# One transformer layer on one core: batch 2's projections reordered in the first pass, work moved between the first two batches, a projection's first matmul ahead of the shift

## What is computed

```python
qkv = layernorm(x) @ qkv_w.T                    # 16 heads of 8 channels
qb, kb = q, k averaged over blocks of 64 rows   # 8 blocks
c = einsum(qb, kb) * scale                      # block against block, per head
mask = (c >= the largest of each row) | own block
probs = softmax(where(mask, q @ k.T * scale, -inf))
x = x + (probs @ v) @ proj_w.T + proj_b
xf = layernorm(x); logits = xf @ wr + br        # 4 experts, the best 2 count
h = gelu(xf @ w1 + b1); y = h @ w2 + b2         # each expert 128 -> 512 -> 128
x = x + sum over the best two of gate * (y - c_sel + c_sum)
```

## Time and profile before

| | us |
|---|---|
| median of 3 runs | 876.28 |
| lowest, highest | 875.84, 877.91 |
| the profiled execution's own time | 867.59 |
| its span (first to last instruction) | 865.6 |

### The profile page before, as it was taken

How to read it: one execution, slowest core, us unless ns; L and a number is a source line. 1 busy time by engine, 2 the same in 40 slices (tenths; PEclk the granted TensorE clock), 3 DMA queues, 4 the chain that set the end, 5 groups by cost and what they waited for, 6 DMA issues and landing times.

```text
span 865.6 us, 23561 instructions
## 1 busy us (share of the span) xinstructions
PE 811.2 (94%) x9326; PEld 546.7 (63%) x9326; DVE 519.5 (60%) x1526; ACT 469.3 (54%) x772; POOL 174.8 (20%) x176
## 2 busy tenths in 40 slices
PE   2668899999999999999999999999999999999995
PEld 2546666666667666666767676666766666665662
DVE  7655647575665756666675757666575666655321
ACT  1334464755557474655637465554747465563740
POOL 6100411213022121303122031212212130201111
PEclk8776999999999999999999999999999999999998
DMA  5989613737566473736557284646647374650210
GB/s 157 226 229 219 151 62 107 164 129 171 136 162 164 128 180 120 179 116 166 141 165 174 97 177 129 165 125 175 167 121 168 122 174 128 166 129 2 62 62 14
DMA packets 187185, 121.90 MB, mean 141 GB/s; under 512 B 123688, under 2 KB 169648, under 8 KB 187072
## 3 DMA queue, kind: packets, MB, share of 16 engines
q1 hardware_dynamic: 184768, 107.77, 48.2%
q0 software_dynamic: 2304, 12.58, 4.8%
HBM read 78.24 MB, written 42.08 MB: 139 GB/s over the span
## 4 chain that ended last, share of the span: by engine, by line
PE 76%; ACT 10%; issue 4%; DVE 4%; DMA 2%; SPq 2%; POOL 0%; POOLq 0%; ACTq 0%; DVEq 0%
PE y_ps L446 20%; PE o_ps L376 8%; PE s_ps L282 6%; PE s_ps L328 6%; PE s_ps L284 5%; PE s_ps L283 5%; PE s_ps L361 5%; ACT hid L1128 5%; PE o_ps L388 4%; PE v_ps L352 3%; PE a_ps L419 2%; ACT L1085 2%; PE v_ps L408 2%; PE v_ps L446 2%; PE v_ps L400 1%
## 5 line engine op out<-in xcount | busy, mean ns | idle before, releaser
L446 PE MATMUL y_ps<-hid,w2s 128*128 128x512 f32 x480 | 235.1, 600 | 0.0
L1085 ACT ACTIVATE prob<-s_ps 128x1024 f32<-128x1024 f32 x128 | 131.1, 1024 | 131.8 <-PE s_ps L361 131.1
L1128 ACT ACTIVATE hid<-s_ps,b1s 128x512 f32<-128x512 f32 x256 | 171.3, 688 | 41.3 <-PE s_ps L284 38.2
L761 DVE TRANSPOSE_TENSOR_REDUCE rmax<-s_ps 128x16 bf16<-128x512 f32 x256 | 168.1, 698 | 39.4 <-PE s_ps L328 39.3
L1251 POOL TENSOR_TENSOR yT<-yT,gate_cols 128x512 f32<-128x512 f32 x48 | 61.4, 1279 | 293.8 <-DVE gate_cols L865 293.4
L282 PE MATMUL s_ps<-xnhi,w1hi 128*128 128x512 f32 x256 | 113.1, 442 | 1.3
L446 PEld LDWEIGHTS y_ps<-hid,w2s 128*128 128x128 f32 x480 | 83.0, 192 | 43.9 <-issue 40.0
L770 DVE TENSOR_REDUCE nmax<-v_ps 128x64 bf16<-128x256 bf16 x128 | 54.1, 423 | 90.5 <-PE v_ps L352 90.4
L284 PE MATMUL s_ps<-xnhi,w1lo 128*128 128x512 f32 x256 | 101.0, 395 | 0.0
L283 PE MATMUL s_ps<-xnlo,w1hi 128*128 128x512 f32 x256 | 100.6, 393 | 0.0
L376 PEld LDWEIGHTS o_ps<-prob,vaug 128*32 128x32 f32 x4096 | 64.5, 111 | 55.2 <-issue 42.4
(11 more groups left out here) (163 smaller groups left out, 1042.5 us busy)
## 6 DMA issues: line engine op xcount, KB each, us to landing
gate_cols<-gates SPq DMA_DIRECT2D x64, 256.0 KB, 4.1
kv_table<-stage SPq DMA_DIRECT2D x16, 768.0 KB, 4.1
keys<-kv_table SPq DMA_DIRECT2D x48, 256.0 KB, 6.6
qdiag<-q_table SPq DMA_DIRECT2D x128, 96.0 KB
kv_chosen<-selected SPq DMA_DIRECT2D x32, 384.0 KB, 4.4
keys<-kv_chosen SPq DMA_DIRECT2D x96, 128.0 KB, 3.3
q_table<-qpair SPq DMA_DIRECT2D x16, 512.0 KB, 2.9
xs<-in_x SPq DMA_DIRECT2D x16, 256.0 KB, 5.6
```

What stands on the lines that cost most here:

```text
L446: ins = pe.matmul(dst[:], w2s[:, n, :], hid[:, n, :], start=(c == 0), stop=(c == C - 1))
L761: v.tensor_reduce(rmax[m % 2][:, :, half * P // 2:half * P // 2 + HH].rearrange("p k h -> p h k"), s_ps[m % 2][:, half * N:(half + 1) * N] ...
L1085: act.activation(prob[m % 2][:].rearrange("p h s -> p (h s)"), s_ps[m % 2][:], ACT.Exp, scale=SCALE).then_inc(exped, 1)
L1128: act.activation(hid[:, k, :], up_ps[up_bank(k)], ACT.Gelu, bias=b1s[:, k:k + 1]).then_inc(gelued, 1)
```

## The change

In `early(0)`: batch 2's k is projected ahead of the steps, q in step 3 and v in step 6 (before: q, then k in step 2, then v in step 4). The readers move with them: DVE takes `ksum` in u = 0, the low half of k in u = 2, `qsum` and the block product's input in u = 4, `qlo` in u = 6; ACT copies k's high half behind step 1 (now with a wait for `k_summed`), q's behind step 4, v behind step 6. `values(0, 0)` moves ahead of `shift(0, 0)`. `begin(1)` (batch 1's first scores and values) and `a_products(2)` now come at the end of step 7, ahead of `weighted(0, 7)`; before, both weighted sums 6 and 7 came first. DVE's `a_select(2)` moves from step 6 to step 7, and `block_max(1, 0)` stands behind it.

In `early(1)`: three of the four `bn_stats` of batch 0's second mean move to step 2, batch 0's route sum to step 7. POOL's `split_w1` now waits for `xn2_done`, that is, until DVE has written batch 0's normalised rows.

On SP: batch 1's `place_q`, both halves, is issued ahead of `put_q(2)` and `put_table(2)`. `take_own(b)` for b >= 3 also waits until POOL has added the second of the sums of two batches back (`summed`).

In the 13 passes: the first matmul of each projection is issued ahead of the step's `shift`, the other two stay where all three were.

```diff
@@ project
+            def project_begin(b, part):
+                was, part_of = bank_a.next(part, b), slice("qkv".index(part) * D, ("qkv".index(part) + 1) * D)
+                pe.wait_ge(bank_a.free, was)
+                pe.matmul(a_ps[:], wqkvhi[:, part_of], xnhi[:], start=True, stop=False)
...
@@ early
-                    if m + 1 < M and u >= 1:
+                    if u == 0:
+                        values(b, m)
+                    elif m + 1 < M:
                         values(b, m + 1)
...
-                    if b == 0 and m in (2, 4):
-                        project(2, "k" if m == 2 else "v")
-                    if b == 0 and m == 6:
+                    if b == 0 and m in (3, 6):
+                        project(2, "q" if m == 3 else "v")
+                    if b == 0 and m == 7:
+                        begin(1)
                         a_products(2)
...
-            project(2, "q")
+            project(2, "k")
             early(0)
-            begin(1)
...
@@ the passes
+                    if ahead and m in stages[:3]:
+                        project_begin(b + 1, "qkv"[stages.index(m)])
                     shift(b, m)
...
                     if ahead and m in stages[:3]:
-                        project(b + 1, "qkv"[stages.index(m)])
+                        project_end("qkv"[stages.index(m)])
...
@@ DVE
+                    if u == 10:
+                        c_stats_begin(0)
...
-                    if b == 0 and m == 6:
+                    if b == 0 and m == 7:
                         tied = a_select(2)
+                        block_max(1, 0)
...
@@ POOL
             inverse(0, mv2, veps2, rstd2, mean2_done, rstd2_done)
+            g.wait_ge(xn2_done, 1)
             split_w1(0)
...
@@ SP
+                if b >= 3:
+                    s.wait_ge(summed, (E - 1) * (b - 3) + 2)
...
+            place_q(1, 0)
+            place_q(1, 1)
             put_q(2)
-            place_q(1, 0)
             put_table(2, bank_a)
-            place_q(1, 1)
```

More of the change, by code:

```diff
@@ L193, in layer @@
         table_out, q_out = sem("table_out"), sem("q_out")
-        q_high, q_summed, own_valued = sem("q_high"), sem("q_summed"), sem("own_valued")
+        q_high, q_summed, k_summed, own_valued = sem("q_high"), sem("q_summed"), sem("k_summed"), sem("own_valued")
         own_k_in, sel_v_in = ([sem(f"{n}{i}") for i in range(2)] for n in ("own_k_in", "sel_v_in"))
@@ L305, in project, with project_end @@
                 exact(dst[:], wqkvhi[:, part_of], wqkvlo[:, part_of], xnhi[:], xnlo[:]).then_inc(of.full, 1)
+            def project_begin(b, part):
+                was, part_of = bank_a.next(part, b), slice("qkv".index(part) * D, ("qkv".index(part) + 1) * D)
+                pe.wait_ge(bank_a.free, was)
+                pe.matmul(a_ps[:], wqkvhi[:, part_of], xnhi[:], start=True, stop=False)
+            def project_end(part):
+                part_of = slice("qkv".index(part) * D, ("qkv".index(part) + 1) * D)
+                pe.matmul(a_ps[:], wqkvhi[:, part_of], xnlo[:], start=False, stop=False)
+                pe.matmul(a_ps[:], wqkvlo[:, part_of], xnhi[:], start=False, stop=True).then_inc(bank_a.full, 1)
             def a_products(b):
@@ L506, in early @@
                     if u == 0:
-                        values(b, m)
                         values(b, m + 1)
@@ L704, in a_q_low, with a_k_early @@
                 v.tensor_tensor(qlo, a_ps[:], qhi.bitcast(F32), ALU.subtract).then_inc(bank_a.free, 1)
-            def a_k_sum(b):
-                v.wait_ge(k_high, b + 1)
-                return step(v.tensor_reduce(ksum[:], block_ap(a_ps[:]), AXX, ALU.add))
+            def a_k_early(b):
+                v.wait_ge(bank_a.full, bank_a.at["k", b])
+                v.tensor_reduce(ksum[:], block_ap(a_ps[:]), AXX, ALU.add).then_inc(k_summed, 1)
             def a_k_rest(b):
@@ L732, in a_qk @@
             def a_qk(total):
-                v.wait_ge(dve_step, total)
+                if total:
+                    v.wait_ge(dve_step, total)
                 v.tensor_tensor(qk[:], heads_of(qsum[:]).broadcast_to([P, M, M]),
@@ L802, in c_stats, with c_stats_begin, c_stats_end @@
                 mean(x2[b % N2], stats2, mv2, mean2_done)
+            def c_stats_begin(b):
+                of = bank_of("proj", b, T - 2)
+                v.wait_ge(of.free, of.at["proj", b, T - 2])
+                for k in range(T - 1):
+                    ins = v.bn_stats(stats2[:, k, :], x2[b % N2][:, k, :])
+                step(ins)
+            def c_stats_end(b):
+                of = bank_of("proj", b, T - 1)
+                v.wait_ge(of.free, of.at["proj", b, T - 1])
+                v.wait_ge(dve_step, step(v.bn_stats(stats2[:, T - 1, :], x2[b % N2][:, T - 1, :])))
+                for k in range(T):
+                    ins = v.bn_aggr(mv2[:, k, :], stats2[:, k, :])
+                ins.then_inc(mean2_done, 1)
             def c_rows(b):
@@ L931, in vector @@
                     if u == 0:
+                        a_k_early(2)
+                    if u == 2:
+                        v.wait_ge(k_high, 3)
+                        a_k_rest(2)
+                    if u == 4:
                         a_q_early(2)
-                    if u == 2:
+                        v.wait_ge(q_summed, 1)
+                        v.wait_ge(k_summed, 1)
+                        a_qk(0)
+                    if u == 6:
                         a_q_low(2)
-                    if u == 3:
-                        k_total = a_k_sum(2)
-                    if u == 4:
-                        a_k_rest(2)
-                        v.wait_ge(q_summed, 1)
-                        a_qk(k_total)
+                    if u == 10:
+                        c_stats_begin(0)
                     if m + 1 < M:
@@ L946, in vector @@
                         o_rows(*pair_at(u - 3))
-                    if b == 0 and m == 6:
+                    if b == 0 and m == 7:
                         tied = a_select(2)
+                        block_max(1, 0)
                     if b == 1 and m == 3:
-                        c_stats(0)
+                        c_stats_end(0)
                     if b == 1 and m == 4:
@@ L954, in vector @@
                         c_split(0)
+                    if b == 1 and m == 7:
                         c_route(0)
-                if b == 0:
-                    block_max(1, 0)
             ranked = c_logits(0)
@@ L1065, in a_q_high, with a_k_high @@
                 act.copy(qhi, a_ps[:]).then_inc(q_high, 1)
-            def a_k_high(b):
+            def a_k_high(b, k_total=False):
                 act.wait_ge(bank_a.full, bank_a.at["k", b])
+                if k_total:
+                    act.wait_ge(k_summed, 1)
                 act.wait_ge(table_out, 16 * b)
@@ L1152, in scalar @@
                     if b == 0 and m == 1:
+                        a_k_high(2, k_total=True)
+                    if b == 0 and m == 4:
                         a_q_high(2)
-                    if b == 0 and m == 2:
-                        a_k_high(2)
-                    if b == 0 and m == 4:
+                    if b == 0 and m == 6:
                         a_v(2)
+                    if b == 0 and m == 7:
+                        values(1, 0)
                     if b == 1 and m == 0:
@@ L1162, in scalar @@
                 o_copy(b, T - 1)
-                if b == 0:
-                    values(1, 0)
             o_columns(1, T - 2)
```

## The result

| | before | after |
|---|---|---|
| median, us | 876.06 (873.52 to 877.91, 4 runs) | 865.20 (864.75 to 865.26, 4 runs) |
| ratio, 95% interval | 1 | 0.9869 (0.984 to 0.9897) |
| profiled execution, own time | 867.59 | 865.26 |
| its span | 865.6 | 863.2 |

The change gains 10.9 us, 2.3 more than the 8.7 forecast and inside the range. But the two profiled executions differ by only 2.4 us. Before's profiled execution took 867.59 us, less than any timed run of that kernel here, the fastest of which took 870.51; after's took what its timed runs take. So the first question is which of the two traces tells of the runs that were timed.

A forecast was written before the change was run, and what follows sets the result against it. PE's own list bounds the kernel from the third pass on, waits and low clock the first two batches. First part 3.5 plus split 5.2 = 8.7 us, from 876.28 to 867.6 us; range 861.5 to 873.7.

The forecast's parts named there:

- first part: Start, batches 0 and 1: its edits, net of w2's lateness and the low clock, gain 3.5 us (1 to 6).
- the split: 13 passes: each projection's first matmul ahead of the shift gains 0.40 us a pass, 5.2 us in all.
- k first: Batch 1's start: the 6.7 us `qpair` wait goes, PE waits 3.8 us for queries, scores at 64.5, before 72.28.
- The select behind begin(1): Batch 1's first scores to next row maximum: 4.5 us instead of 2.21, a loss; row maximum at 69.0.
- w1's split later: Batch 1's step 5: DVE's normalisations no longer slowed by POOL; 2.6 us plus 1.1 of clock, 3.7 gained.
- w2 as the limit: At `bias_out`: w2's load lands at 100.8, PE stands 3.6 us, gain there 5.6 us instead of 9.2.
- rival A: At `bias_out`: w2 in time, start keeps 9.2 us, 861.9; middle (w2 at 99, stand 1.5 us) 864.2; chance 0.2.
- The clock: Behind PE's stand for w2: low clock for 4.2 us of PE work costs 2.1 us (1.2 to 2.7).
- SP's wait: Passes: own keys go out 3.9 us later, chosen keys have 3.8 us to spare; effect 0.
- The rival C: Passes: chosen keys come too late after SP's wait, first scores wait; 883.2 at 5 us delay; chance 0.06.
- B: Passes gain nothing, moved matmul's long slot or DVE's chain: 872.8 (chance 0.18); longer slot loses 2.6 us, 875.4 (0.08).
- D: Start gains nothing: batch 1's queries late, clock low, w2 later by 3 us; total 871; chance 0.1.

The follow-up runs named there:

- before's second trace: The unchanged kernel before, profiled once more: own time 875.94 us.
- first part alone: After with projections whole behind the shift and own keys sent for as in before, so neither edit of the passes: 870.09 us, 0.9933 of before.
- short hold: POOL's gather of chosen rows held until DVE has written head group 6's row maxima: before 864.96 us, after 856.18, after with projection whole 858.77.

## Why the prediction was right, and where it was not

The forecast was -8.7 us and the change brought -10.9. It was carried from one trace to the median, and that trace, as found above, was not typical. Most parts went the way that was forecast (w2 did not), but that the sum came out near is in part luck: the first part brought some 2 to 3 us more than its 3.5, the split 1.4 to 2.6 less than its 5.2, and about 2.5 us of shorter stalls stand in no term.

- **k first.** Right. The `qpair` wait went, ACT's copy of k is at 43.85 (forecast 43.5), and what came is the forecast wait for the queries: 4.2 us against 3.8, scores at 65.38 against 64.5. But its value was overstated: 6.7 us was the long case, 3.3 the usual one.
- **The select behind begin(1).** Right: row maximum at 69.69 against 69.0.
- **w1's split later.** Right in mechanism, undersized: 3.7 us forecast, of which 1.1 for the clock; 5.0 measured, with the 2.7 us stall back as it was when the edit is undone.
- **w2 as the limit.** A step that failed in size. It was to be issued 2.0 us later than before, because the table of batch 2 moved behind the queries. The table did go later (65.44 against 64.18, 1.3 us), but w2 was issued at 90.15, 1.9 us *earlier* than at 92.07: the gather of batch 2 began 1.5 us later and was ready for SP's next DMA 8.3 us after its start (72.27 to 80.58) instead of 11.8 (70.73 to 82.48). The chain behind SP's order was the gather's landing. PE stood 1.5 us for w2 and not 3.6; with 99.47 against a forecast 100 to 101 it lies between the forecast and rival A, near the middle case that A's paragraph names. Over all nine traces of kernels with the new first part even that is much: four show no wait for w2 at all, the others 0.4 to 2.5 us. The wait that all nine have is that for batch 1's queries, 4.2 to 6.5 us. It, and not w2, is the limit that is left, and that the `bias_out` of after came near the forecast time is in part its doing.
- **The clock.** The low clock foreseen behind w2's stand did not come (1.00 from 81 us on). It came where I had not priced it, behind the wait of 4.20 us for the queries:

```profile
66.00:71.00 5.00, 3.05 (x44) 2.57 (x42) 3.43 (x12) 0.85 (x2) 0.00 (x0) 0.50 0.99 301
71.00:76.00 5.00, 4.51 (x47) 3.45 (x46) 3.01 (x6) 3.25 (x6) 0.96 (x1) 0.50 1.16 307
```

In all of 60 to 90 us the mean granted clock is 0.77 in after and 0.90 in before's second trace, in 36 to 60 us 0.95 and 0.85: a loss and a gain of which the sum holds neither.

- **First part, 3.5 us.** Timed runs give 5.4 (first part alone) and 865.0 - 858.8 = 6.2 (both with the short hold). Inside the 1 to 6 given but for 0.2. 5.0 of the 6.2 hang on the wait for `xn2_done`; the new order of k, q and v with the select behind begin(1) was not run alone, and by difference it is left with about 1.2. The traces' 7.0 was too much by the unusual start.
- **The split, 5.2 us.** The mechanism is right, the size is off: 0.29 us a pass, 3.8 in all by the trace and 2.6 timed. The step that failed is the slot of 0.23 us ahead of the shift; it is 0.33, and the text had priced that case at 0.30 a pass, 3.9 us. (By its own terms it should have been 0.42 - 2 x 0.08 = 0.26, 3.4 us.) I chose the wrong one of my two ends: the slot followed the four short score matmuls, and the first projection matmul after short ones had taken 0.32. The room ahead of the shift was sized wrong as well, 0.25 and 0.15 us and not 0.30 and 0.20. By steps the forecast was 0.24, 0.18 and 0, the gain 0.17, 0.06 and 0.06: in step 4 DVE's chain did not take back what step 3 gained.
- **SP's wait, nothing.** Right of the wait as such: nothing in before, nothing with the gather held. In after as it stands the medians give it 3.0 us, with the projection whole 0.7, and the trace of the former puts the difference into the first part. What the traces do show is that own keys sent for ahead of the gather go with longer stalls behind it: up to 1.3 us, against 1.1. How much of the 3.0 us is that stays open.
- **The rival C** did not come: no pass waits for its chosen keys. **B** and **D** neither. The rule on row groups (0.19 us more a step) is answered by the split's gain in all three steps and by the slot of 0.33 us; the moved matmul's neighbours are 96 and 64 rows high in these fences, not 128 as the text has it.
- **Not seen at all:** 10 to 12 us in stalls behind the gather, in before and after alike. The trace that I read had 1.6 us of them, too little to stand out. Its own time, 8.2 us *under* the fastest of the three times given (867.59 against 875.84), was the sign, and I explained nothing with it.

How PE's news is held back stays open. The runs show that it goes with the gather's start, that the held signals come 1.3 to 1.6 us behind that start in after and up to 0.9 in the unusual trace of before, and that PE loses nothing by it when the gather starts 1.8 us later in the step. They do not show what in the gather does it, nor whether it is POOL's instruction or the DMA traffic that it starts, nor why that one execution was nearly spared.

## What to carry to other kernels

Compare the profiled execution's own time with the timed ones before building on it: where it lies under all of them, it is another case than the one you are asked about, and a second profile costs little. When several engines start together after work that the trace shows as long done, look for what another queue began just before, and move it to where no engine waits for such a result; here one wait on POOL brought 9 to 12 us, about as much as the whole change. And price a moved matmul by the slot it has in its new company, not in its old.

## What the hardware showed that was not expected

- Signals of PE that fell due just behind the start of a GpSimd-issued gather were raised together, in after 1.3 to 1.6 us behind that start in 13 of 13 passes, while DVE's were on time. PE lost by it 0.4 to 1.3 us in 10 to 13 of the 13 passes in all traces but before's first one and those with the gather held. With the same gather 1.8 us later in the step it lost nothing, because no signal of PE fell due then.
- DVE's two-input operation L855 (128x64) took 0.22 us alone, 1.81 beside a gather and a sum on GpSimd, 1.18 beside the sum.
- After 2.71 us of waiting PE's granted clock was 0.50, 0.82 and 0.66 in the three stretches up to 108 us; the wait on POOL that removes this stall is worth 5.0 us timed, nearly twice the stall. After the 1.5 us of waiting for w2 in after it stayed at 1.00.
